# A gated cross-attention and feed-forward block on one core: SP's transfers reordered in attention, weight jobs three blocks apart, signed tiles stored from where they lie

## What is computed

```python
q, k, v = split(LN(x) @ w_q), split(ctx @ w_k), split(ctx @ w_v)
a = softmax(q @ k.T * SCALE + causal_mask) @ v
x = x + tanh(g_xattn) * (merge(a) @ w_o)

def act_qdq(x):      # 16 bits, one scale for the whole tensor
    scale = max(max(abs(x)) / 32767, 1e-12)
    return clip(round(x / scale), -32768, 32767) * scale

def ffn(x, w_gate, w_up, w_down):      # lpbq: 4 bits, a scale for each 32 weights
    x = act_qdq(x)
    up = act_qdq(x @ lpbq(w_up).T)
    gate = act_qdq(x @ lpbq(w_gate).T)
    sig = round16u(sigmoid(gate))
    gate = act_qdq(gate * sig)
    return act_qdq(gate * up) @ lpbq(w_down).T

x = x + tanh(g_ffn) * ffn(LN(x), w_gate, w_up, w_down)
```

## Time and profile before

| | before |
|---|---|
| median of 3 timed runs | 1364.98 us (1361.59 to 1366.13) |
| profiled execution | 1364.77 us |
| its span, first to last instruction | 1362.7 us |
| PE busy | 1226.6 us, 90% |
| DVE busy | 991.0 us, 73% |
| ACT busy | 676.7 us, 50% |
| POOL busy | 289.1 us, 21% |
| mean granted clock of PE | 0.959 of full speed |

### The profile page before, as it was taken

One profiled execution on the slowest core, in us unless ns is written; L12 is line 12 of the kernel. 1 busy time (PEld: TensorE's weight loads), 2 busy tenths in 40 slices (PEclk: granted clock), 3 DMA queues, 4 the chain that ended last, 5 costly groups with the idle time before them and its releaser, 6 DMA issues. The chain is left out here.

```text
span 1362.7 us, 18913 instructions
## 1 busy us (share of the span) xinstructions
PE 1226.6 (90%) x5889; PEld 594.7 (44%) x5889; DVE 991.0 (73%) x1430; ACT 676.7 (50%) x789; POOL 289.1 (21%) x375
## 2 busy tenths in 40 slices
PE   7999799899899989999999899999991079999998
PEld 6644544444354444444444344444440034444443
DVE  3779589678767667767777499978998974545554
ACT  3533343344344334444443388858977964334341
POOL 0246326425534321212111033110110000000000
PEclk9999899899999999999999899999996589999999
DMA  9123333433434448788887999964578974555553
GB/s 339 40 59 92 106 102 92 110 89 105 119 93 123 132 146 245 227 241 260 241 248 188 274 321 340 334 223 175 196 252 314 410 250 158 183 192 209 181 205 103
DMA packets 205356, 262.91 MB, mean 193 GB/s; under 512 B 112880, under 2 KB 125168, under 8 KB 205296
## 3 DMA queue, kind: packets, MB, share of 16 engines
q1 hardware_dynamic: 205008, 262.21, 59.5%
q10 hardware_dynamic: 288, 0.00, 0.0%
HBM read 143.13 MB, written 97.52 MB: 177 GB/s over the span
## 5 line engine op out<-in xcount | busy, mean ns | idle before, releaser
L1412 PE MATMUL gpG<-xph,Wh 128*128 128x512 f16 x384 | 147.3, 383 | 5.1 <-ACT gst L1311 4.2
L1412 PE MATMUL gpG<-xph,Wl 128*128 128x512 f16 x384 | 147.1, 383 | 0.0
L1412 PE MATMUL gpG<-xpl,Wh 128*128 128x512 f16 x384 | 147.0, 383 | 0.0
L1986 PE MATMUL pD<-Wh,xph 128*128 128x512 f16 x384 | 145.5, 379 | 1.0 <-DVE xpl L1961 1.0
L1412 PE MATMUL pU<-xph,Wh 128*128 128x512 f16 x384 | 146.0, 380 | 0.0
L1412 PE MATMUL pU<-xpl,Wh 128*128 128x512 f16 x384 | 146.0, 380 | 0.0
L1412 PE MATMUL pU<-xph,Wl 128*128 128x512 f16 x384 | 145.9, 380 | 0.0
L1986 PE MATMUL pD<-Wl,xph 128*128 128x512 f16 x384 | 145.5, 379 | 0.0
L1986 PE MATMUL pD<-Wh,xpl 128*128 128x512 f16 x384 | 145.5, 379 | 0.0
L1311 ACT ACTIVATE gst<-gpG,rw 128x512 f32<-128x512 f32 x96 | 65.6, 684 | 119.4 <-PE gpG L1412 58.7
L1344 DVE TENSOR_REDUCE gmx<-gst 128x512 f32 (+1 forms) x96 | 65.2, 679 | 62.3 <-ACT gst L1311 62.1
(11 more groups left out here) (242 smaller groups left out, 2621.1 us busy)
## 6 DMA issues: line engine op xcount, KB each, us to landing
dub<-up_d SPq DMA_DIRECT2D x42, 768.0 KB, 4.8
gate_d<-gst SPq DMA_DIRECT2D x96, 256.0 KB, 3.4
gb<-gate_d SPq DMA_DIRECT2D x24, 768.0 KB, 7.0
up_d<-ust SPq DMA_DIRECT2D x72, 256.0 KB, 4.1
eu<-up_d SPq DMA_DIRECT2D x22, 768.0 KB, 6.6
xr<-xn_d SPq DMA_DIRECT2D x9, 1024.0 KB, 6.4
xin<-in_x SPq DMA_DIRECT2D x32, 256.0 KB, 3.5
x_d<-x SPq DMA_DIRECT2D x32, 256.0 KB, 2.5
```

The source lines that it names most:

```text
L1412: mm = pe.matmul(ps[:, :], Ws[:, it, kt * P:(kt + 1) * P], xs[:, kt, :], start=(kt == 0 and Ws is Wh and xs is xh), stop=(kt == KT - 1 and ...
L1986: mm = pe.matmul(pD[4 * t + q][:, :], os_[n][:, cs], Ws[:, it, :], start=(it == 0 and os_ is oh and Ws is Wh), stop=(it == IT - 1 and os_ ...
```

## The change

Four things are changed; the arithmetic and its results are the same.

**1. SP in attention.** The blocks of SP's step change places: first the x transposes (now of tile k+1, since they stand a step later), then the job's store and its transposes, then the stores of tile k-3, then the job's load.

```diff
-                j = k - 3
-                if have(j):
-                    ...
-                if have(k + 2):
-                    j = k + 2
+                if have(k + 1):
+                    j = k + 1
                     sp.wait_ge(*tile(xl_done, b, j))
...
                     for part_, to in zip((J.hi[q % 2], J.lo[q]), turned[q % 2]):
                         sp.dma_start_transpose(blocks_of(to), part_[:, :]).then_inc(turn_in[q % 2], 16)
+                j = k - 3
+                if have(j):
+                    ...
```

```diff
-                    if it == 3 and not (last and t):
+                    if it == 2 and not (last and t):
...
-                    if it in (5, 9, 11):
+                    if it in (5, 8, 10):
...
-                        if it == 1 and not (last and t):
+                        if it == 0 and not (last and t):
...
-                        if it in (3, 7, 11):
+                        if it in (3, 6, 9):
...
-                        if it % 4 == 1:
+                        if it in (1, 4, 7):
...
-                        if it % 4 == 3:
+                        if it in (3, 6, 9):
```

```diff
-AWAY = range(0, QT, 2)
+AWAY = range(0, QT - 2, 2)
...
-                    for k in away[j, it]:
-                        sp.wait_ge(f_done, k + 1)
-                        sp.dma_start(f_d[AWAY.index(k - QT), :, :], f_away).then_inc(f_out, 16)
+                    for n in away(j, it, 3):
+                        sp.wait_ge(f_done, QT + AWAY[n] + 1)
+                        sp.wait_ge(f_out[n % 2], 16 * (n // 2))
+                        sp.dma_start(f_d[n, :, :], nq[:, AWAY[n], :]).then_inc(f_out[n % 2], 16)
...
-                    for k in away[j, it]:
-                        act.wait_ge(f_done, k + 1)
-                        act.activation(nq[:, k - QT, :], f_away, ACT.Abs).then_inc(f_abs, 1)
+                    for n in away(j, it, 5):
+                        act.wait_ge(f_done, QT + AWAY[n] + 1)
+                        act.wait_ge(f_out[n % 2], 16 * (n // 2 + 1))
+                        act.activation(nq[:, AWAY[n], :], nq[:, AWAY[n], :], ACT.Abs).then_inc(f_abs, 1)
...
-                to = nq[:, k - QT, :]
-                if k - QT in AWAY:
-                    to, n = f_away, AWAY.index(k - QT)
-                    if n:
-                        dve.wait_ge(f_abs, n)
-                        dve.wait_ge(f_out, 16 * n)
-                dve.scalar_tensor_tensor(out=to, in0=nq[:, k - QT, :], scalar=C_F, in1=mb[k % NM][:, :],
+                dve.scalar_tensor_tensor(out=nq[:, k - QT, :], in0=nq[:, k - QT, :], scalar=C_F, in1=mb[k % NM][:, :],
```

**4. More of the sigmoid's integers on GpSimd**, every second k of the second half (16) instead of every fourth (8):

```diff
-            return k >= QT and k % 4 == 3
+            return k >= QT and k % 2 == 1
```

More of the change, by code:

```diff
@@ L161, in flamingo_block @@
             d_unit = sb(ff, "d_unit", [P, H], F32)
-            x_rows = sb(ff, "x_rows", [P, 2 * H], F32)
-            x_row = [x_rows[:, n * H:(n + 1) * H] for n in range(2)]
-            f_away = x_rows[:, :].bitcast(I16)[:, 0:I]
+            x_row = [sb(ff, f"x_row{n}", [P, H], F32) for n in range(2)]
             load_w = [lambda eng, c, d=d, s=s: load_weights(eng, W, d, s, c) for d, s in zip(wsc, w_in)]
@@ L600, in step @@
                         sp.dma_start_transpose(blocks_of(to), part_[:, :]).then_inc(turn_in[q % 2], 16)
+                j = k - 3
+                if have(j):
+                    n = j % 2
+                    sp.wait_ge(*tile(x1_done, b, j))
+                    sp.sem_inc(J.apart, 1)
+                    sp.dma_start(x1_d[bass.ds(S * b + j * P, P), :], x1[n][:, :]).then_inc(x1_out[n], 16)
+                    if have(j + BQ):
+                        sp.dma_start(xin[j % BQ][:, :], xf[bass.ds(S * b + (j + BQ) * P, P), :]).then_inc(x_in[j % BQ], 16)
+                    sp.wait_ge(*tile(x2_done, b, j))
+                    sp.sem_inc(J.apart, 1)
+                    sp.dma_start(xn_d[bass.ds(S * b + j * P, P), :], x2[n][:, :]).then_inc(x2_out[n], 16)
+                if not jobs and b == B - 1:
+                    if k == 3:
+                        sp.wait_ge(ch_ps, NCH * B)
+                        for n in range(2):
+                            sp.wait_ge(*at(J.stored[n], 0, 32 * 12 // J.NJ))
+                            sp.wait_ge(*at(x2_out[n], 0, 16 * BQ // 2))
+                    if 3 <= k < 7:
+                        load_gate(sp, k - 3)
+                    if 7 <= k < 9:
+                        sp.dma_start(xr[k - 7][:, :, :], four_tiles(xn_d, k - 7)).then_inc(xr_in[k - 7], 16)
                 q = job_at(k, jobs, 1)
@@ L1208, in traffic @@
                     sp.dma_start(dst.rearrange("a p k -> (a p) k"), stage[n][:, :]).then_inc(st_out[n], 16)
-                    if it == 3 and not (last and t):
+                    if it == 2 and not (last and t):
                         sp.wait_ge(*at(xl_done, 2 * KT * i, KT * t))
+                        sp.sem_inc(apart, 1)
                         for q in range(4):
@@ L1457, in up_phase @@
         xp_in = [sem(f"u_xp_in{n}", 16 * 2 * KT) for n in range(2)]
-        f_out, f_abs = sem("u_f_out"), sem("u_f_abs")
+        f_out, f_abs = [sem(f"u_f_out{n}") for n in range(2)], sem("u_f_abs")
         d_ps, d_set, n_act = sem("u_d_ps"), sem("u_d_set"), sem("u_n_act")
@@ L1480, in up_phase, with away @@
         due = {(m // IT, m % IT): [k for k in range(2 * QT) if slot_of(k) == m - 1 - m_by_pool(k)] for m in range(FT * IT)}
-        away = {(m // IT, m % IT): [k for k in range(QT, 2 * QT) if k - QT in AWAY and slot_of(k) + 3 == m] for m in range(FT * IT)}
+        def away(j, it, later):
+            return [n for n, g in enumerate(AWAY) if slot_of(QT + g) + later == IT * j + it]
         def freed(eng, k):
@@ L1815, in load_f @@
                     sp.dma_start(fr[n % 2], f_d[n, :, :]).then_inc(fr_in[n % 2], 16)
-                sp.wait_ge(f_out, 16 * len(AWAY))
+                sp.wait_ge(f_abs, len(AWAY))
                 for g in AWAY[0:2]:
```

15 lines of the change are left out of this document (8 added, 7 removed).

## The result

The changed kernel takes **1326.9 us** (median of 4, 1325.3 to 1328.5) against 1365.4 before; the ratio is 0.972, 95% interval 0.970 to 0.975.

| stretch | before | after | difference | forecast |
|---|---|---|---|---|
| start to the gate stage's first product | 508.7 | 484.8 | -23.9 | -19.3 |
| gate stage, first to last product | 258.3 | 250.5 | -7.8 | -5.9 |
| barrier behind it, with its filler | 8.5 | 5.8 | -2.7 | -4.2 |
| up stage, with the clock behind the barrier and the wait at its end | 260.8 | 256.4 | -4.4 | -9.4 |
| to the first down product | 72.3 | 73.3 | +1.0 | +1.0 |

The account below looks back on a forecast made before the run. TensorE, the busiest engine, was taken as the bound, so gains come only from its idle time and clock: 13.6 + 4.5 + 1.2 + 5.9 + 6.1 + 7.5 - 1.0 = 37.8 us, 1364.8 to 1327.0 us; range 1319 to 1345.

Parts of the forecast that it names:

- VectorE's three idle times of 4.5: Attention: VectorE's row sums idle for ScalarE's exponentials, behind late job transposes; all three counted as gained, 13.6 us.
- the first batch's clock: Attention: clock behind TensorE's first large wait, of which 2.2 us would remain; credited with nothing (up to 2 us).
- the low halves: Attention: TensorE's 2.4 us of waits for VectorE's low halves; bounds 0 and 2.4, half taken, 1.2 us.
- The clock rival: Attention, gate stage, barrier: clock not given back or followers eat it; 4.5, 1.2, 1.7, 1.9 stay out, 1336 us; chance 0.22.
- The 1.9 behind the barrier: Barrier behind the gate stage: wait falls to 1.7 us, so the lowered clock behind it goes too, gaining 1.9 us.
- the 4.2 us: Gate stage: TensorE's two waits for a staging tile, up to 2.4 us, would go, gaining 4.2 us.
- can leave at 767.05 + 0.69 = 767.7: End of gate stage: last block's store leaves then, turned stores right behind; SP ends at 770.3, gaining 4.2 us.
- A magnitude now waits for a DMA that was issued two blocks (5.2 us) earlier: End of up stage: a store landing in 3.4 us is hidden; magnitudes waiting for their stores would show the prediction wrong.
- 7.5 us: End of up stage: TensorE's wait behind the last up block falls from 9.4 us to near 1.9, gaining 7.5.
- the rival (0.10): Up stage: each of GpSimd's eight new multiplications stops VectorE for its whole 1.92 us; 1332 us; chance 0.10.
- 3.2 us for eight more instructions: Up stage: contention cost on VectorE of GpSimd's eight new multiplications, taken as 3.2 us, with a slack of 6.7.
- First pass of the down stage: Start of down stage: VectorE's 37 passes end some 2.0 us later, TensorE's filler covers 1.1; cost 1.0 us.

## Why the prediction was right, and where its terms were not

- **Attention, mechanism and places: right.** No high half waits for a job's transpose, VectorE's three idle times of 4.5 in front of its row sums are 1.2 at most, TensorE's waits 2.1 and less. The edit of the transposes alone carries it. Terms too small: the first batch's clock (2.1, credited with 0) and the low halves (about 2.4, of which I took half). Both had been named as bounds, and the bound was what came; for the clock that is luck of the execution, since it fell behind the same wait in two of nine traces.
- **The clock rival (0.22): refuted in attention, half true at the barrier.** It was given back in attention in full. The 1.9 behind the barrier wasn't in this execution; it was with six blocks, where the wait was the same. The step that failed is "The wait falls to 1.7, like the 1.77 that kept the clock": the wait was 3.2, and behind such a wait the clock is a matter of the execution.
- **Gate stage: right in kind, 1.9 too small.** All staging waits went. The term that was mis-sized is the 4.2 us: it took the two long waits from the list, where TensorE's starts have seven stops of 5.7 us. Another 0.5 came from the clock at the start of the stage. Which of the stage's moves did it (rows, jobs, transposes) wasn't run apart.
- **The barrier: the step that failed is that the last block's store "can leave at 767.05 + 0.69 = 767.7".** I had taken the queue behind it and not the transposes ahead of it. 3.2 us instead of 1.7; the kernel with less for SP to do there measured 1.8.
- **End of the up stage: the step that failed is "A magnitude now waits for a DMA that was issued two blocks (5.2 us) earlier".** VectorE's product, and with it the store, came later than the table has it, by all of that distance, and the store was issued 0.5 us after ScalarE was ready to overwrite the tile. 4.2 of 7.5 us came; one block more of distance brings 3.3 of the missing. That was one of the things I had named that would make the prediction wrong.
- **GpSimd on VectorE: the rival (0.10) is refuted,** and my own price was wrong too: 3.2 us for eight more instructions, where the loss grew by 0.9 against before and not at all against the changed kernel with eight. The rule of "SBUF — State Buffer" in the Trainium skill ("Who interferes with whom"), by which one of the two is shut out for the whole instruction, doesn't show as a loss of that size on VectorE here. That GpSimd is the one shut out isn't excluded: its instruction grew by 0.7 us.
- **First pass of the down stage: right,** +1.0 with 37 passes, covered as forecast.

So the forecast of 1327.0 rests on errors that cancel: 6.5 us too little in attention and the gate stage, 6.5 too much at the two stage ends.

The version that beats both kernels is the changed one with the magnitudes six blocks behind: 1323.6 us.

## What to carry to other kernels

When an in-order queue is late, look first for one transfer whose data was ready long ago; two transposes moved forward gave 23 of 38 us here. For a buffer that is stored and then overwritten in place, take the distance from the end of the instruction that fills it in the trace, not from its slot in a table: an engine that runs full is late against its slots. And where an issue "can leave" at some time, list what stands ahead of it on its queue, at the last tile above all.

## What the runs showed that was not expected

- The same wait of TensorE (2.09 to 2.10 us) left the granted clock at 1.00 in seven traces and let it fall in two, to 0.57 and 0.62 over the next 4 us; 3.2 to 3.6 us gave both as well. A single trace therefore doesn't tell what a stop costs.
- GpSimd's multiplication of 128x1536 beside VectorE went from 1.87 to 2.60 us when there were sixteen and not eight, while VectorE's own loss didn't follow the number: 3.2 to 4.4 us in six traces with eight, 4.1 to 4.2 in four with sixteen and 1.1 in the two with sixteen and six blocks.
- A job's transposes had to be followed by three blocks of 2.6 us before SP touched their result; with two, SP waited up to 2.2 us for their landing, twelve times.
